# Gates stored and loaded ahead of the second half of the expert weights, and transposed two products earlier, in a fused cross-attention and mixture-of-experts layer

## What is computed

```python
x = x + tanh(g_ffn) * ffn(layernorm(x))
def ffn(x):                          # flat: 1024 tokens of 256
    shared = sum(relu(x @ sw1[i] + sb1[i]) @ sw2[i] + sb2[i] for i in range(2)) / 2
    probs = softmax(x @ router_w + router_b)          # 32 experts
    topk_p, topk_i = top_k(probs, 6); topk_p /= sum(topk_p)
    gates = zeros(1024, 32).at[rows, topk_i].add(topk_p)
    routed = sum(gates[:, e] * (relu(x @ rw1[e] + rb1[e]) @ rw2[e] + rb2[e]) for e in range(32))
    return shared + routed           # hidden width 176 per expert
```

## Time and profile before

| | |
|---|---|
| median of 3 runs | 475.64 us |
| the profiled execution | 475.44 us |
| its span, first to last instruction | 473.6 us |
| outside the span | 1.84 us |
| PE busy | 448.4 us, 95% of the span |
| DVE, ACT, POOL busy | 286.7, 199.0, 144.1 us |
| mean granted clock of PE | 0.989 of full speed |
| chain that ended last, by engine | PE 85%, DVE 7%, ACT 3%, DMA 2%, issue 1%, POOL 1% |

### The profile page before, as it was taken

One profiled execution on the slowest core, in us unless ns is written; L12 is line 12 of the kernel. 1 busy time (PEld: TensorE's weight loads), 2 busy tenths in 40 slices (PEclk: granted clock), 3 DMA queues, 4 the chain that ended last, 5 costly groups with the idle time before them and its releaser, 6 DMA issues.

```text
span 473.6 us, 8151 instructions
## 1 busy us (share of the span) xinstructions
PE 448.4 (95%) x2515; PEld 335.4 (71%) x2515; DVE 286.7 (61%) x574; ACT 199.0 (42%) x366; POOL 144.1 (30%) x233
## 2 busy tenths in 40 slices
PE   5788999999999998888899999999999999999996
PEld 5356666666666665566688888888888888888885
DVE  7897977877777674640445555455554455554455
ACT  1467777787877565471222222222222222222221
POOL 9046800000000000245144333444333444334430
PEclk9799999999999999999899999999999999999999
DMA  8012111111111100999852323333223322334102
GB/s 220 15 47 48 35 32 34 35 32 32 30 32 35 24 1 11 329 333 316 205 150 89 89 89 100 116 93 89 89 89 111 110 89 89 89 93 125 48 0 90
DMA packets 34056, 43.62 MB, mean 92 GB/s; under 512 B 5633, under 2 KB 28209, under 8 KB 34033
## 3 DMA queue, kind: packets, MB, share of 16 engines
q1 hardware_dynamic: 30737, 42.07, 31.1%
q10 hardware_dynamic: 3296, 1.25, 1.1%
HBM read 37.93 MB, written 1.18 MB: 83 GB/s over the span
## 4 chain that ended last, share of the span: by engine, by line
PE 85%; DVE 7%; ACT 3%; DMA 2%; issue 1%; POOL 1%; DVEq 0%; SPq 0%; POOLq 0%; ACTq 0%
PE psum L1126 26%; PE psum L1111 26%; PE psum L962 8%; PE psum L975 7%; PE psum L938 6%; PE psum L925 3%; PE psum L949 2%; PE psum L881 2%; PE psum L1024 2%; PE psum L890 1%; DVE nmax L716 1%; DVE ang L619 1%; PE psum L853 1%; PE psum L986 1%; DMA G<-gates_by_expert 1%
## 5 line engine op out<-in xcount | busy, mean ns | idle before, releaser
L591 ACT ACTIVATE hh<-hu 128x512 fp32r<-128x512 f32 x88 | 55.6, 633 | 186.7 <-DVE hu L822 186.7
L822 DVE SCALAR_TENSOR_TENSOR hu<-psum,b1cols,G 128x512 f32<-128x512 f32 x88 | 65.9, 751 | 110.3 <-PE psum L1111 101.3
L716 DVE TENSOR_REDUCE nmax<-psum 128x2 f32<-128x512 f32 x128 | 85.2, 687 | 25.9 <-PE psum L938 24.6
L492 ACT ACTIVATE probs<-psum 128x512 f32<-128x512 f32 x128 | 69.4, 595 | 14.1 <-PE psum L962 13.7
L1126 PE MATMUL psum<-hh,w2h 128*128 128x512 f32 (+1 forms) x188 | 73.3, 390 | 1.3 <-DVE hl L828 1.3
L1126 PE MATMUL psum<-hl,w2h 128*128 128x512 f32 (+1 forms) x188 | 73.2, 389 | 0.0
L1126 PE MATMUL psum<-hh,w2l 128*128 128x512 f32 (+1 forms) x188 | 73.1, 389 | 0.0
L828 DVE SCALAR_TENSOR_TENSOR hl<-hu,hh 128x512 fp32r<-128x512 f32 x88 | 60.3, 687 | 9.6 <-ACT hh L591 9.6
L1111 PE MATMUL psum<-xTh,w1h 128*128 128x512 f32 (+1 forms) x188 | 58.8, 394 | 2.2 <-POOL w1l L405 1.5
L1111 PE MATMUL psum<-xTh,w1l 128*128 128x512 f32 (+1 forms) x188 | 58.8, 394 | 0.0
L1111 PE MATMUL psum<-xTl,w1h 128*128 128x512 f32 (+1 forms) x188 | 58.5, 392 | 0.0
(11 more groups left out here) (148 smaller groups left out, 550.3 us busy)
## 6 DMA issues: line engine op xcount, KB each, us to landing
G<-gates_by_expert SPq DMA_DIRECT2D x40, 256.0 KB, 3.9
w<-in_L_ffn_rw_dram SPq DMA_DIRECT2D x4, 1408.0 KB, 13.4
w<-in_L_ffn_rw_dram SPq DMA_DIRECT2D x2, 2816.0 KB, 17.5
G<-gates_by_expert SPq DMA_DIRECT2D x8, 448.0 KB, 3.5
Kd<-QK SPq DMA_DIRECT2D x104, 32.0 KB, 1.9
G<-gates_by_expert SPq DMA_DIRECT2D x8, 384.0 KB, 3.5
G<-gates_by_expert SPq DMA_DIRECT2D x8, 320.0 KB, 3.4
G<-gates_by_expert SPq DMA_DIRECT2D x8, 192.0 KB, 3.7
```

Of the source, the lines that this page charges most:

```text
L492: act.activation(probs[g % 2][:, kt, 2 * hp:2 * hp + 2, :], ST_BANK[(4 * g + n) % 3][:, :].rearrange("p (h q) -> p h q", h=2), ACT.Exp, sc ...
L591: act.activation(hh[(SHT + j) % 2][:, cols], hu[2 * j + half][:, :], ACT.Relu).then_inc(rhh_ok, 1)
L716: dve.tensor_reduce(nmax[i % 2][:, qt, 2 * hp:2 * hp + 2], S_BANK[n % 2][:, :].rearrange("p (h k) -> p h k", h=2), AX.X, ALU.max, negate=T ...
L822: dve.scalar_tensor_tensor(out=hu[2 * (j % 2) + half][:, :], in0=H_BANK[2 * (j % 2) + half], scalar=b1cols[:, bass.ds(it * len(G) + j, 1)] ...
```

## The change

It adds a semaphore `hl2_ok` and has these parts. On SP the weights' second half is issued after the G of the first four tiles. On PE `gates_transposed` moves from behind `hidden(3)` to behind `hidden(2)`, and `result(1)` stands behind it. On ACT the relu of u = 1 moves in front of the exponential, and the copy of the first half of `gTf` in front of the third shared tile. The low parts of u = 2 to 5 move from POOL to DVE, u = 2, 3 in front of DVE's copy of `gTf` and u = 4, 5 behind it. POOL waits for all normalised rows before its `xTl`. One `tensor_scalar` of the inverse deviation becomes a `scalar_tensor_tensor` with a constant tile, which a memset fills at the start.

```diff
@@ sync @@
-            for c in range(2):
+            def load_weights(c):
...
+            load_weights(0)
             for half in range(2):
                 cols = slice(half * HALF, (half + 1) * HALF)
                 sp.wait_ge(gTf_ok[half], 1)
                 sp.dma_start(gd[:, cols], gTf[0:NE, cols]).then_inc(gd_st, 16)
             sp.wait_ge(gd_st, 32)
             for r in range(RT):
+                if r == len(G):
+                    load_weights(1)
                 if r >= len(G):
                     sp.wait_ge(hu_ok, 2 * (r - len(G)) + 2)
@@ gpsimd @@
+            pool.wait_ge(xn2_ok, NT)
             for b in (0, 2, 3):
...
-            for u in range(2 * SHT):
+            for u in range(2):
                 shared_low_part(u)
@@ scalar @@
-            def shared_hidden(u):
+            def shared_relu(u):
...
-                if u >= 2:
+                if t == 1:
                     act.wait_ge(hl_ok, u - 1)
+                if t == 2:
+                    act.wait_ge(hl2_ok, u - 3)
...
-            shared_hidden(0)
+            shared_relu(0)
+            shared_high_part(0)
+            shared_relu(1)
             act.wait_ge(sub_ok, 1)
             act.activation(ex[:, :, :], ex[:, :, :], ACT.Exp).then_inc(pexp_ok, 1)
-            for u in range(1, 2 * SHT):
-                shared_hidden(u)
+            shared_high_part(1)
+            for u in range(2, 4):
+                shared_relu(u)
+                shared_high_part(u)
             act.wait_ge(gT_mm, 1)
             act.activation(gTf[:, 0:HALF], GT_BANK[0][0:NE + NS, :], ACT.Copy).then_inc(gTf_ok[0], 1)
+            for u in range(4, 6):
+                shared_relu(u)
+                shared_high_part(u)
@@ vector @@
+            then(dve.memset(three_halves[:, :], 1.5))
...
-                then(dve.tensor_scalar(newton[:, rows], newton[:, rows], -0.5, 1.5, ALU.mult, ALU.add))
+                then(dve.scalar_tensor_tensor(out=newton[:, rows], in0=newton[:, rows], scalar=-0.5,
+                                              in1=three_halves[:, rows], op0=ALU.mult, op1=ALU.add))
...
+            def shared_low_part(u):
...
+                dve.wait_ge(hh_ok, u + 1)
+                dve.tensor_tensor(hl[t % 2][0:rows, cols], hr[half][0:rows, :], hh[t % 2][0:rows, cols],
+                                  ALU.subtract).then_inc(hl2_ok, 1)
+            shared_low_part(2)
+            shared_low_part(3)
             dve.wait_ge(gT_mm, 2)
             dve.tensor_copy(gTf[:, HALF:TOK], GT_BANK[1][0:NE + NS, :]).then_inc(gTf_ok[1], 1)
+            shared_low_part(4)
+            shared_low_part(5)
@@ tensor @@
-            for t in range(SHT - 1):
-                hidden(t + 1, t + 1, P if t + 1 < SFULL else SREST)
-                result(t, t, P, first=(t == 0)).then_inc(y_mm, 1)
-            hidden(SHT, SHT % 2, P, pair=0, r=0)
...
+            hidden(1, 1, P)
+            result(0, 0, P, first=True).then_inc(y_mm, 1)
+            hidden(2, 2, SREST)
             pe.wait_ge(gates_ok, 1)
             pe.wait_ge(half_ok, 1)
             gates_transposed(0)
             gates_transposed(1)
+            result(1, 1, P).then_inc(y_mm, 1)
+            hidden(SHT, SHT % 2, P, pair=0, r=0)
             result(SHT - 1, SHT - 1, SREST).then_inc(y_mm, 1)
```

More of the change, by code:

```diff
@@ L96, in gated_cross_attention_moe @@
         newton = sb("newton", [P, NT])
+        three_halves = sb("three_halves", [P, NT])
         wout_sb = sb("wout_sb", [P, KD, D])
@@ L213, in gated_cross_attention_moe @@
             sem(n) for n in ("half_ok", "ws_hi", "ws_ok", "h_mm", "relu_ok", "hh_ok", "hl_ok", "y_mm", "act_sync", "pool_sync"))
+        hl2_ok = sem("hl2_ok")
         hu_ok, rhh_ok, rhl_ok = (sem(n) for n in ("hu_ok", "rhh_ok", "rhl_ok"))
@@ L542, in shared_hidden, with shared_high_part @@
                 act.wait_ge(h_mm, u + 1)
-                if u >= 2:
+                if t == 1:
                     act.wait_ge(hl_ok, u - 1)
+                if t == 2:
+                    act.wait_ge(hl2_ok, u - 3)
                 act.activation(hr[half][0:rows, :], H_BANK[half][0:rows, :], ACT.Relu,
                                bias=b1half[0:rows, t:t + 1], scale=1.0 / NS).then_inc(relu_ok, 1)
+            def shared_high_part(u):
+                t, half = u // 2, u % 2
+                rows = P if t < SFULL else SREST
                 if t >= 2:
@@ L810, in _ @@
             dve.tensor_tensor(gates[:, :, 0:NE], sel[:, :, :], per_expert(red[:, 1]), ALU.mult).then_inc(gates_ok, 1)
+            def shared_low_part(u):
+                t, half = u // 2, u % 2
+                rows = P if t < SFULL else SREST
+                cols = slice(half * HALF, (half + 1) * HALF)
+                dve.wait_ge(hh_ok, u + 1)
[3 more added lines that the diff above has]
+            shared_low_part(3)
             dve.wait_ge(gT_mm, 2)
             dve.tensor_copy(gTf[:, HALF:TOK], GT_BANK[1][0:NE + NS, :]).then_inc(gTf_ok[1], 1)
+            shared_low_part(4)
+            shared_low_part(5)
             with dve.Fori(0, RT // len(G)) as it:
@@ L1117, in result @@
                 for half in halves:
-                    if isinstance(t, int) and t < SHT:
-                        pe.wait_ge(hl_ok, t * 2 + half + 1)
+                    if isinstance(t, int) and t == 0:
+                        pe.wait_ge(hl_ok, half + 1)
+                    elif isinstance(t, int) and t < SHT:
+                        pe.wait_ge(hl2_ok, t * 2 + half - 1)
                     else:
```

## The result

The changed kernel takes 469.0 us (median of 4 runs, 466.33 to 469.12) against 475.35 us (474.84 to 475.83, 4 runs) before: a ratio of 0.9857, 95% interval 0.9824 to 0.989. The forecast was 470.4 us, with a range of 468.0 to 473.8.

A forecast was written before the change was run, and what follows sets the result against it. PE was taken as the bound, busy nearly throughout, so only gaps and low-clock work could go: 1.7 + 0.4 + 1.6 of gaps and 1.3 of the last wait, together 5.05 with rounding, giving 470.4 us, range 468.0 to 473.8.

The forecast's parts named there:

- the case that was forecast: Clock falls behind the eight bias matmuls, `hidden(4)` takes 4.6 us, `result(3)` starts at 228.1; 470.4 us, chance 0.5.
- Part 1: Last block's transposes: with POOL waiting for the normalised rows they start at 196.6 in place of 198.34, -1.7 us.
- The feared wait for `xTl`: Rival: late `xTl` on POOL makes `hidden(0)` wait 1.3 us, so part 1 gives nothing; 471.7 us, chance 0.07.
- Part 2: Relu of u = 1 ahead of the exponential: 0.74 gap goes, about 0.5 new wait in `result(0)`; -0.4 us.
- Part 3: Low parts of u = 2 to 5 on DVE: the 1.47 gap before the first routed `w1l` goes, -1.6 us.
- Parts 4 and 5: Transposes behind `hidden(2)`, cost 0; store takes 3 us, first G issued about 215.3, landed 220.0, off the path.
- Part 6: Weights' second half ahead of G of tile 4: G lands about 246.5, wanted at 247.15; cost 0, bound 4.7 us.
- its slack of 0.6 us: Margin between G of tile 4 landing and being wanted; rival that it is late: 471.5 to 475 us, chance 0.17.
- a long wait of DVE for this G: Sign that the prediction is wrong: DVE waiting long for G of tile 4; no such wait was expected.
- the first rival: Clock holds behind the bias matmuls, `result(3)` could start at 226.2; 469.7 us, down to 468.5; chance 0.2.

The follow-up runs named there:

- second profile: The changed kernel profiled again with no edit; 469.8 us (4 runs), ratio to before 0.9864.
- first profile: The changed kernel's own first profiled execution, the fastest of its four runs; 466.33 us.
- the order alone: The kernel before with only SP's order changed, the weights' second half behind G of tile 3; 478.64 us, ratio 1.0054.
- third profile: The changed kernel unedited, run again on one chip with the version of pieces and split bias matmuls; 469.23 us (5 runs), ratio 0.9856.
- weights first: The changed kernel with both halves of the weights issued at the start again; 477.67 us, ratio to before 1.0029.
- POOL free: The changed kernel without POOL's wait for the normalised rows, the new instruction form kept; one run, 470.17 us.

## Why the prediction was right

The terms came out near where they were put, and with them the total of the case that was forecast, the one in which the clock falls. The second profile shows that case, and it shares its start with the kernel before (first product at 40.43 and 40.35), so its times can be set beside the forecast's:

| step | forecast | second profile |
|---|---|---|
| last block's transposes | 196.6 | 196.75 |
| wait inside `result(0)` | 0.5 | 0.30 |
| gate transposes | 210.6 | 210.93 |
| first G issued | 215.3 | 214.17 |
| bias matmuls | 219.9 | 219.93 |
| `hidden(4)` takes | 4.6 | 4.55 |
| `result(3)` | 228.1 | 228.17 |
| span | 468.55 | 468.4 |

- **Part 1** (1.7 us): measured 1.7 by taking POOL's wait away. The feared wait for `xTl` did not come: DVE's `xTl` went first in all three profiles of the changed kernel (193.45 against POOL's 193.62 in the first). The rule of the Trainium skill (SBUF — State Buffer, "Who interferes with whom") that two SBUF inputs contend with a POOL instruction that reads SBUF is borne out: the `scalar_tensor_tensor` took 1.26 us beside POOL's `xTl` and 0.16 without it.
- **Part 2** (0.4): measured 0.4 by undoing it.
- **Part 3** (1.6): right, though the weights' first half landed later than forecast. In the second profile POOL waited for it until 209.0, 12 us after L1112, where 206.3 was forecast: 21.4 us from the first issue (187.62), where the sum took 17.8 us from 188.5. `hidden(3)` was not due before 214.5, so the slack took that. Undone alone, the part costs 4.6 us, not 1.6: 2.8 us of wait, since the moved `gTf` copy pushes ACT's relus back, and 1.85 us of low clock behind it.
- **Parts 4 and 5**: the store was quicker (2.2 us from its first issue to G's first, 3 were taken), G landed about 5 us after its issue (4.7).
- **Part 6**: right in kind, and its slack of 0.6 us was not met in any profile. G of tile 4 landed 31.7 us after the first G's issue in the first profile (211.44 to 243.17), 32.0 in the order alone, 29.9 in the third profile (212.78 to 242.7, taken as 0.25 us before DVE's start in the line below, the distance in the first profile) and at most 30.6 in the second, where DVE no longer waited for it at 244.75; the forecast was 31.2. Wanted 19.05 us behind the start of `result(3)`, it is 0.2 us late in the first profile, 1.5 us early in the third and at least 2.4 us early in the second. So that `result(7)` is on time in two of the three, and 0.4 us late in the first, is in part luck of a landing that varies by 2 us. The prediction named a long wait of DVE for this G as a sign that it is wrong. The sign appears (6.33 us in the first profile, 4.59 in the third), but it was badly chosen: PE lost 0.4 us in the one and nothing in the other.

```profile
242.97 1.41 DVE L853 SCALAR_TENSOR_TENSOR hu<-psum,b1cols,G 128x512 f32<-128x512 f32 x2 [4.59 <-DMA G<-gates_by_expert]
```

  The rule that descriptors are taken in the order of the ring (the Trainium skill, DMA: Bandwidth & Descriptors, "Queues, rings and completion order") is borne out from both sides, by the store behind the weights (weights first) and by G behind them (the order alone).
- **The clock**: the forecast case and the first rival both occur, in different executions of one kernel. Eight bias matmuls in a row had a fall behind them in 7 of 11 profiles (in POOL free from the last 0.5 us of them on), four and four in none of 3. The rule that ties a fall to idling (the Trainium skill, TensorE: Matmul & The Clock Gate, "HAM oscillation — how this bites in real kernels") fits the falls behind PE's waits of 5.64, 4.26, 3.49 and 2.79 us, but not the one behind the bias matmuls, where PE was busy for 3.70 of 3.70 us. Why they let it fall was not settled. That breaking them up helps is likely and not proven: unbroken, 4 of 11 profiles had no fall, and at that rate three in a row without one come by chance about once in twenty times. The timed runs point the same way. In the profiles a mean clock of 0.991 or more goes with no fall after the first 40 us and one of 0.990 or less with a fall; it was 0.991 or more in 14 of 17 timed runs with the matmuls split, and in 5 of 13 of the changed kernel. But 0.989 occurs in 3 runs with the split too, of which no trace was kept, so that the split always holds the clock is not shown.

Where the sum was off: the median, 469.0, lies 1.4 us under the forecast. Some executions hold their clock, and some have a shorter start. The forecast took the start of the kernel before for granted, and nothing in it allowed for either share; which has how much of the median can't be said from mean clocks alone.

## What to carry to other kernels

A transfer that is not urgent costs by what stands behind it in the queue: count what is issued behind it, up to the first one that somebody waits for, and hold the landing against the pace of the consumer. An order of transfers can be a gain or a loss according to when the first of them can start, so it is to be changed together with the compute that feeds it. And a wait that disappears may have hidden a stretch at a low clock; look at the granted clock under every wait that a change removes.

## What the runs showed of the hardware beyond that

The start of the span comes in two forms, whatever the kernel does later. DVE's first `tensor_scalar` on 16 elements per partition, beside POOL's memsets, in the changed kernel's first profile:

```profile
4.29 0.87 DVE L637 TENSOR_SCALAR ang<-pos_sb 128x16 f32<-128x16 f32 x1 [1.28 <-DMA pos_sb<-in_fside_BxSx_dram]
```

and in the second, same code:

```profile
4.37 8.04 DVE L637 TENSOR_SCALAR ang<-pos_sb 128x16 f32<-128x16 f32 x1 [1.35 <-DMA pos_sb<-in_fside_BxSx_dram]
```

It took 0.75 to 0.92 us in 6 of the 14 profiles, 7.87 to 8.22 us in 7, and 5.45 us in the kernel before. The long ones end with one of POOL's memsets: at 12.41 in the second profile, where a memset ends at 12.39, and at 9.66 in the kernel before, where one ends at 9.64. That POOL holds the instruction over several memsets is likely from this, and not tested. When it starts does not decide it: in the order alone it also started at 4.29, and took 8.13 us. After the long form the sine starts at 13.89 in place of 11.63, 2.3 us later.

The rest of the difference is the clock. In every profile PE waits 3.8 to 6.2 us for `ctxT` in the start, the clock falls in that wait or just behind it, and the eight matmuls that follow take 5.25 to 6.70 us, by how long it stays low. In the first profile and the third, both of the short form:

```profile
12.91 5.40 PE L912 MATMUL psum<-wkv_sb,ctxT 128*128 128x512 f32 x8 [4.11 <-ACT ctxT L440]
```

```profile
12.90 6.70 PE L912 MATMUL psum<-wkv_sb,ctxT 128*128 128x512 f32 x8 [3.99 <-ACT ctxT L440]
```

The granted clock from 13.0 to 18.0 was 0.66 and 0.50. The first attention product starts 19.4 us behind the end of these matmuls in all 14 profiles, so the 2.7 us between the first profile and the second are 2.3 of the form and 0.4 of the clock (5.83 us for these matmuls in the second). No run here took the memsets away; 2.3 us, where the long form occurs, is what these profiles let one hope for.

Waits of PE cost more than their length. Behind the waits of 2.79 to 5.64 us in the changed stage the next `hidden` or `result` ran at 1.2 GHz for most of its length and took 1.8 to 2.7 us more; behind those of 1.47 and 1.80 us in the kernel before there was no such fall.
